# Decoder layer: the router's logits computed one iteration later and at another place, key chunks of 128 instead of 121

## What is computed

```
x = layernorm(x + windowed_self_attention(x))           # 4 heads of 64
x = layernorm(x + cross_attention(x, ctx_1024))         # 16 heads of 16, 361 keys
x = layernorm(x + moe(x))                               # 8 experts, top 2

def cross_attention(query, ctx):
    Q, K, V = (proj(query, wq, bq), proj(ctx, wk, bk), proj(ctx, wv, bv))
    energy = einsum('bhqd,bhkd->bhqk', Q, K) / 4
    out = einsum('bhqk,bhkd->bhqd', softmax(energy), V)
    return out.reshape(B, S, 256) @ wo.T + bo

def moe(xt):
    logits = xt @ Ws + bs                               # 256 -> 8, from the second layernorm's result
    topk_w, topk_idx = top_k(logits, 2)
    ...                                                 # silu(x Wg) * (x Wu), then Wd, weighted
```

## Time and profile before

| | us |
|---|---|
| median of 3 runs | 747.06 |
| lowest, highest run | 745.37, 747.82 |
| the profiled execution, its time | 747.7 |
| its span, first to last instruction | 745.9 |
| TensorE (PE) busy with matmuls | 653.6 |
| loads of stationary operands (PEld) | 517.9 |
| VectorE (DVE) busy | 379.6 |
| ScalarE (ACT) busy | 318.7 |
| GpSimd (POOL) busy | 259.8 |

### The profile page before, as it was taken

The page is one execution under the profiler, slowest core; times in us unless marked ns, Lnnn a source line. Parts: engine busy times, 40 slices in busy tenths (PEclk is TensorE's granted clock), DMA queues, the critical chain, the costliest instruction groups (busy, mean ns, idle before and its releaser), DMA issues. The chain is left out here.

```text
span 745.9 us, 15440 instructions
## 1 busy us (share of the span) xinstructions
PE 653.6 (88%) x5196; PEld 517.9 (69%) x5197; DVE 379.6 (51%) x897; ACT 318.7 (43%) x757; POOL 259.8 (35%) x462
## 2 busy tenths in 40 slices
PE   6998976999999999999997266999999999999940
PEld 5888864677777777777775164777777777777730
DVE  2877885777777777777772461222222222222213
ACT  2344342677776777777765002222222222222204
POOL 3334553333344333334321102333343343343123
PEclk9999987999999999999998556999999999999985
DMA  8232115556556555555552530121112111112015
GB/s 233 87 75 79 46 44 148 140 156 174 178 150 189 166 160 162 158 158 158 140 156 67 219 130 29 22 32 34 28 30 36 28 28 37 25 28 35 13 27 149
DMA packets 61146, 73.72 MB, mean 99 GB/s; under 512 B 7769, under 2 KB 52129, under 8 KB 60321
## 3 DMA queue, kind: packets, MB, share of 16 engines
q1 hardware_dynamic: 54944, 65.48, 29.9%
q0 software_dynamic: 6144, 7.48, 6.1%
HBM read 38.25 MB, written 12.39 MB: 68 GB/s over the span
## 5 line engine op out<-in xcount | busy, mean ns | idle before, releaser
L1032 DVE TENSOR_REDUCE cmx<-ps 100x1 f32<-100x361 f32 x256 | 133.8, 532 | 74.0 <-PE ps L576 71.9
L835 ACT ACTIVATE cpr<-ps 121x300 f32<-121x300 f32 x256 | 105.1, 420 | 53.5 <-PE ps L587 52.7
L1544 DVE TENSOR_TENSOR hh<-sg,ps 128x344 f32<-128x344 f32 x64 | 32.8, 513 | 131.4 <-PE ps L1354 131.4
L587 PEld LDWEIGHTS ps<-st 120*121 120x121 bf16 x768 | 81.8, 137 | 20.1 <-issue 5.8
L1292 POOL DMA_INDIRECT accd<-y,si x32 | 51.3, 1604 | 124.9 <-DVE y L1555 124.9
L576 PE MATMUL ps<-st 96*100 96x361 bf16 x256 | 85.7, 338 | 5.7 <-DMA st<-parts 3.3
L1376 PE MATMUL ps<-WD,hT 128*128 x384 | 88.3, 380 | 1.3 <-ACT hT L1420 1.3
L1354 PE MATMUL ps<-WG,xsT 128*128 x256 | 86.0, 459 | 0.6 <-ACT xsT L1409 0.6
L587 PE MATMUL ps<-st 120*121 120x100 bf16 x768 | 82.8, 217 | 2.4 <-ACT st L840 1.6
L1354 PE MATMUL ps<-WU,xsT 128*128 x256 | 84.8, 454 | 0.0
L1376 PEld LDWEIGHTS ps<-WD,hT 128*128 128x128 f32 x384 | 72.8, 190 | 16.0 <-issue 1.8
(11 more groups left out here) (189 smaller groups left out, 1078.8 us busy)
## 6 DMA issues: line engine op xcount, KB each, us to landing
st<-parts SPq DMA_DIRECT2D x192, 115.2 KB, 2.4
WD<-in_wd SPq DMA_DIRECT2D x6, 1024.0 KB, 10.4
cx<-in_ctxT SPq DMA_DIRECT2D x16, 361.0 KB, 5.2
WG<-in_wg SPq DMA_DIRECT2D x8, 688.0 KB, 5.2
WU<-in_wu SPq DMA_DIRECT2D x8, 688.0 KB, 4.7
x_sb<-in_x SPq DMA_DIRECT2D x8, 200.0 KB
x1d<-x SPq DMA_DIRECT2D x8, 200.0 KB
x1Td<-x1T SPq DMA_DIRECT2D x8, 200.0 KB, 3.3
```

The costliest lines, as they stand in the source:

```text
L587: mm = pe.matmul(ps[0:CM, B_T + h % 2, c * L:(c + 1) * L], st[b % NX][:, h, c * CH:c * CH + CM], st[b % NX][:, h, CTX:KQ], start=True, sto ...
L835: act.activation(pr[:, h % (2 * HG), :], ps[0:CM, B_T + h % 2, 0:NCH * L], ACT.Exp).then_inc(exp_ok, 1)
L1032: dve.tensor_reduce(mx[:, half, hh:hh + 1], ps[0:L, B_S + h % 2, 0:CTX], AX_X, ALU.max).then_inc(max_ok, 1)
L1544: dve.tensor_tensor(hh[:, t.par, f * FH:(f + 1) * FH], sg[:, f, :], ps[:, B_U + f, 0:FH], ALU.mult).then_inc(h_ok, 1)
```

## The change

It has two parts that don't need each other.

1. **The logits move.** `logits(i - 2)` runs at head 12 of iteration i (from i = 2), ahead of `turn_maximum(i+1, 0)`, so one iteration later than before. Its result lies in bank M1, in columns 100 to 107 beside the turned maxima (columns 0 to 99), instead of M2. `logits_out(i - 2)` runs at head 13 on ScalarE, behind `maximum_out(i+1, 0)` and ahead of the exponential of head 14. Only the last batch's logits stay at head 15, in iteration 16. The waits follow: `logits` waits for the eviction of the first two value chunks (v_ev up to 2b + 7), for the last logits' eviction and for an older `maximum_out`; `keys(b, 1)`, which writes M1, waits for lg_ev; `queries` and `turn_maximum(b, 1)`, which write M2, no longer do; `x2T_out(b)` waits until the logits that read x2T before are done.

2. **The chunks have 128 keys.** They begin at 0, 128 and 233. The middle one overlaps the last: of its 128 keys 105 are used. Tiles cpr and cva and the PSUM rows take 128 partitions. The number of instructions is as before, but for the order.

```diff
-CH = (CTX - 1) // NCH
-CM = CH + 1
+FROM = (0, P, CTX - P)
+USED = (P, CTX - 2 * P, P)
...
                     for c in range(NCH):
-                        mm = pe.matmul(ps[0:CM, B_T + h % 2, c * L:(c + 1) * L],
-                                       st[b % NX][:, h, c * CH:c * CH + CM], st[b % NX][:, h, CTX:KQ],
+                        mm = pe.matmul(ps[:, B_T + h % 2, c * L:(c + 1) * L],
+                                       st[b % NX][:, h, FROM[c]:FROM[c] + P], st[b % NX][:, h, CTX:KQ],
                                        start=True, stop=True)
...
                     for c in range(NCH):
-                        n = CH if c < NCH - 1 else CM
+                        n = USED[c]
...
                         pe.wait_ge(q_ev, min(b + 3, NB))
-                        wait(pe, lg_ev, b - 1)
...
                         wait(pe, mT_ev[0], b - 1)
+                        wait(pe, lg_ev, b - 4)
...
                     pe.wait_ge(x1T_in[b % 2], 16 * (b // 2 + 1))
-                    wait(pe, lg_ev, b - 3)
...
-                        mm = pe.matmul(ps[0:CM, bank, o:o + D], cx[b % NX][:, k, c * CH:c * CH + CM], wv_sb[:, k, :],
+                        mm = pe.matmul(ps[:, bank, o:o + D], cx[b % NX][:, k, FROM[c]:FROM[c] + P], wv_sb[:, k, :],
...
                 def logits(b):
                     pe.wait_ge(x2T_ev, b + 1)
-                    pe.wait_ge(v_ev, min(2 * b + 6, 2 * NB))
-                    pe.wait_ge(mT_ev[1], min(b + 2, NB))
+                    pe.wait_ge(v_ev, min(2 * b + 7, 2 * NB))
+                    wait(pe, lg_ev, b)
+                    pe.wait_ge(mT_ev[0], min(b + 3, NB))
                     for k in range(KC):
-                        mm = pe.matmul(ps[0:L, M2, 0:E], x2T[:, k, :], ws_sb[:, k, :],
+                        mm = pe.matmul(ps[0:L, M1, L:L + E], x2T[:, k, :], ws_sb[:, k, :],
...
+                        if h == 12 and i >= 2:
+                            logits(i - 2)
                         if h == 12 and s:
                             turn_maximum(i + 1, 0)
...
-                        if h == 15 and tail:
+                        if h == 15 and i == NB:
                             logits(i - 1)
...
                 def x2T_out(b):
                     act.wait_ge(x2T_mm, b + 1)
+                    wait(act, lg_mm, b)
...
+                        if h == 13 and i >= 2:
+                            logits_out(i - 2)
-                        if h == 15 and tail:
+                        if h == 15 and i == NB:
                             logits_out(i - 1)
```

More of the change, by code:

```diff
@@ L112, in __init__ @@
         self.own = sb("own", [SR + MR, H])
-        self.va = [sb(f"cva{u}", [CM, NCH, H, VC]) for u in range(2)]
+        self.va = [sb(f"cva{u}", [P, NCH, H, VC]) for u in range(2)]
         self.sources = ((self.wk, wkT), (self.wq, wqT), (self.wv, wvT), (self.wo, woT), (self.ws, ws),
@@ L237, in attention @@
         parts = sb("parts", [P, KC, SLOTS, KQ], BF16)
-        pr = sb("cpr", [CM, 2 * HG, NCH * L])
+        pr = sb("cpr", [P, 2 * HG, NCH * L])
         oT = sb("oT", [P, NG, L])
@@ L834, in exps @@
                         wait(act, pv_mm, NG * b + h // HG - 1)
-                    act.activation(pr[:, h % (2 * HG), :], ps[0:CM, B_T + h % 2, 0:NCH * L], ACT.Exp).then_inc(exp_ok, 1)
+                    act.activation(pr[:, h % (2 * HG), :], ps[:, B_T + h % 2, 0:NCH * L], ACT.Exp).then_inc(exp_ok, 1)
                 def maximum_out(b, half):
@@ L867, in values_out @@
                         act.activation(va[b % 2][:, 0:2, :, 0:DH],
-                                       ps[0:CM, M1, :].rearrange("p (c h d) -> p c h d", c=2, h=H),
+                                       ps[:, M1, :].rearrange("p (c h d) -> p c h d", c=2, h=H),
                                        ACT.Copy).then_inc(v_ev, 1)
@@ L872, in values_out @@
                         act.activation(va[b % 2][:, 2, :, 0:DH],
-                                       ps[0:CM, M2, 0:D].rearrange("p (h d) -> p h d", h=H),
+                                       ps[:, M2, 0:D].rearrange("p (h d) -> p h d", h=H),
                                        ACT.Copy).then_inc(v_ev, 1)
@@ L892, in logits_out @@
                     act.wait_ge(lg_mm, b + 1)
-                    act.activation(LG[:, b:b + 1, :], ps[0:L, M2, 0:E].unsqueeze(1), ACT.Copy).then_inc(lg_ev, 1)
+                    act.activation(LG[:, b:b + 1, :], ps[0:L, M1, L:L + E].unsqueeze(1), ACT.Copy).then_inc(lg_ev, 1)
                 projections(0)
```

## The result

The changed kernel takes 735.75 us (median of 4 runs, 731.97 to 737.27) against 746.21: a ratio of 0.986, 95% interval 0.9828 to 0.9891. Run again beside the kernel before it took 735.35 against 746.57, ratio 0.9846 (0.9822 to 0.9869). The direction was right; the amount was not: 5.6 us were forecast.

The account below looks back on a forecast made before the run. TensorE was taken to bound cross-attention, not by matmuls alone. Logits' move 4.7 + 0.65 + 0.27 = 5.6 us, chunks 0: 747.7 - 5.6 = 742.1, in medians 741.5; range 737.5 to 744.7.

Parts of the forecast that it names:

- What bounds the stage: Cross-attention, full iteration of 17.85 us: TensorE bounds it with 17.21 us of matmuls, but not by its matmuls alone.
- the 0.80 us at head 15: TensorE at head 15: logits' matmul L687 waits for ScalarE's copy L888 and starts 0.80 us late.
- Part 1, the boundary: Logits' move, iterations 2 to 13: key projection L628 starts 0.39 us earlier per boundary, twelve boundaries giving 4.7 us.
- the last boundaries: Logits' move, late iterations: 0.27 us gained from 14 to 15, 0 in iteration 15, nothing in 16.
- its stated ends: Logits' move in iteration 15: forecast gain 0, with ends -0.3 and +0.2 us.
- Part 2: Chunks of 128 keys: price taken as 0, between 0.8 us more and 2.5 us less.
- the cheap end: Key loads L587 taking no time of their own: three scores 0.02 us shorter per head, 2.5 us less in all.
- The rival of the fast load: Loads L587: at exactly 128 columns the load drops out of the scores' chain, 2.5 us less, total 739.0; chance 0.34.
- the price of 0.02 per head: Three key scores take 0.14 to 0.15 us instead of 0.16 to 0.17, counted for 9 heads in 14 iterations.
- The clock: Half-clock stretch of 3.4 us behind iteration 14: one such stretch more or less is 1.7 us.
- The copy: Rival: logits' copy L893 ahead of head 14's exponential costs up to 0.47 us; at 0.4, total 745.4; chance 0.11, with other partial losses.
- The wait at head 12: Rival: logits wait for L867, which has 0.09 us to spare; ending 0.7 later gives 749.9 us; chance 0.04.

Follow-up runs that it names:

- the move alone: The changed kernel with the old chunks of 121 keys at 0, 120 and 240, so only the logits' place differs from before: 739.6 us, ratio 0.9912.

## Why the prediction missed

- **What bounds the stage, and the 0.80 us at head 15: right.** The wait is gone from head 15, and the iteration shortened by what the distances of starts gave.
- **Part 1, the boundary: right, and slightly short.** 0.39 us per boundary were worked out, 0.41 measured (17.85 to 17.44). Each link shows up about where it was put: 0.08 for the logits' copy (0.06 to 0.07 where it was moved away), the exponential of head 14 as the next late thing, L628 0.78 behind it (0.75 taken from iteration 0). That only half of the visible stall would return was right. Two small misses cancel: at head 12 the logits push by 0.33 (316.45 to 316.78 with the move alone) and not 0.37, and L628 comes 0.03 later than taken. At the last boundaries the sum was nearly right with the wrong parts: iteration 14 gave 0.42 and not 0.27, and iteration 15 cost 0.23, within its stated ends, where 0 was taken. In the whole, 5.6 were given; the traces show 5.75 and the medians 6.6 (5.0 to 8.1). The prediction didn't name VectorE's maximum, which stands next behind the exponential at the boundary, with only 0.16 us between them.
- **Part 2: this is the step that failed.** The sum took a price of 0 for the wider load, "between the ends and nearer to the 121-column row". Measured: 4.3 us less (2.8 to 5.8), in the trace 3.5, beyond the cheap end of 2.5. The fault was to treat the load's time as one line in the number of columns. Two rows, at 100 and 121 columns, always lie on a line and can't tell a step from none. The load of 127 (138 ns) is still near it, the next column leaves it. The rival of the fast load had the mechanism, the direction and nearly the size: 0.22 us per iteration against 9 x 0.02 = 0.18. The Trainium skill (TensorE: Matmul & The Clock Gate, section Weight-path perf modes) puts the fast load at 128 weights and a type other than FP32. The trace now agrees: 101 ns at 128, 138 at 127.
- **The price of that rival was too low, too:** 2.5 us against 3.5 in the trace and 4.3 by the medians. The price of 0.02 per head was right: over the groups of three scores that nothing holds up it is 0.136 from the first start to the next instruction's, where it was 0.157. What was short is the count. A full iteration gave 0.22, or ten to eleven heads and not nine, and only 14 of the 16 iterations with such scores were counted, while 14 and 15 gave 0.17 and 0.31. In these two, exponentials and scores wait for each other in turn, so that a shorter group of scores would shorten each round; this reason is argued, the two gains are measured. Its own sum of 739.0 was too high as well.
- **The clock: right as an uncertainty, wrong as a suspicion.** The stretch at half clock in the first profile made its execution 1.2 us longer, where 1.7 was taken, and didn't come again. The profiled execution of the changed kernel (731.97) happened to be its fastest, so the two first profiles differ by 16.5 us in span while the medians differ by 10.5. An account drawn from these two alone would have had 6 us too much to explain.
- **The range.** With the fast load and part 1 at what the traces show, 3.5 and 5.75, the sum from 747.06 is 737.8, just inside the range. With both at what the medians show, 4.3 and 6.6, it is 736.2. The kernel before, run more often, came to 746.2 to 746.8, which is 0.3 to 0.9 lower. So the failed step makes up most of the miss of 5.8 us, a lower start a little, and about 1 us stays open, as said above. The low end of 737.5 left no room for both terms being somewhat larger at once.
- **The other rivals.** The copy cost 0.08 us and not 0.4. The wait at head 12 never came: L687 starts right behind its scores, 0.13 behind their start.

## What to carry to other kernels

When a tile comes near the full width of an engine's unit, two rows below that width don't give the price at it: one build with the full width and one with a column less settle it in two runs. Removing a wait gives only what the next late thing leaves; follow the queue of the engine that was late, by distances of starts, to see how much. And work of no urgency (here the logits, the first of them copied at 177 us and read at 405) belongs where its engine waits anyway, in another engine's shadow, with its copy out of the chain that sets the pace.

## What the runs showed of the hardware

- The load of a bf16 stationary operand: 126 to 127 ns at 100 columns, 136 to 137 at 121, 138 at 127, and 101 at 128, in all five kernels with 128 columns. So here a load of 128 columns takes less time than one of 100.
- The gain per head in TensorE's queue is smaller than the 36 ns of the load: three scores to the next instruction take 0.13 to 0.14 instead of 0.16 to 0.17 us. One score starts 0.046 behind the last, near the 0.042 that 100 columns take at full clock; that the matmuls then set the distance fits, but isn't shown.
- Of two profiles of one program, one had 3.4 us at half clock in a stage where the other had none; it cost 1.2 us.
- At 128 columns of bf16 the trace's record of the load reads its source as four runs of 32 columns; at 127 and fewer, and at 128 of f32, as one.
